# Eight PSUM banks shared out anew between score products, turns and layer 3 in a four-layer cross-attention kernel

## What is computed

```python
x = L0(x, ctx)      # inorm, 1x1 convs, softmax(Mn^T Mm) over 256 channels, Ml A, conv Wo, + x
x = L1(x, ctx)      # 32 query heads, 8 key heads of 8; softmax; out @ Wo + x; layernorm
x = L2(ctx, x)      # latents = x; 16 heads of 16 over [ctx, x]; out proj + x; rmsnorm;
                    # gelu(out @ w1 + b1) @ w2 + b2 + x
x = L3(x, ctx)      # RWKV block: token shift, mixes, r k v g w, a scan over 64 tokens
                    # for 8 x 8 states, group norm, output proj; then a channel-mix ffn
```

## Time and profile before

| | us |
|---|---|
| median of 3 runs | 1959.85 (1957.9 to 1962.85) |
| profiled execution, its span from first to last instruction | 1957.6 |
| PE busy / DVE / ACT / POOL | 1663.1 / 1235.2 / 939.7 / 812.5 |
| mean granted clock of TensorE | 0.931 of full speed |

### The profile page before, as it was taken

How to read it: one execution, slowest core, us unless ns; L and a number is a source line. 1 busy time by engine, 2 the same in 40 slices (tenths; PEclk the granted TensorE clock), 3 DMA queues, 4 the chain that set the end, 5 groups by cost and what they waited for, 6 DMA issues and landing times.

```text
span 1957.6 us, 36688 instructions
## 1 busy us (share of the span) xinstructions
PE 1663.1 (85%) x13615; PEld 1032.1 (53%) x13615; DVE 1235.2 (63%) x2121; ACT 939.7 (48%) x1855; POOL 812.5 (42%) x903
## 2 busy tenths in 40 slices
PE   5888898889997898898987989978998889888735
PEld 3565555565563655555554645646455465556203
DVE  3743478645786468844786457854688546973483
ACT  4454554545554445545544455544555544453202
POOL 4531248404573147702485034830467113760070
PEclk8998999998999899998998989989999989999857
DMA  6001014200331005100141102310052000410070
GB/s 179 2 2 35 1 20 53 45 18 1 44 41 33 18 1 67 24 27 18 18 55 34 29 1 36 49 34 18 1 61 30 27 18 9 59 24 13 1 87 11
DMA packets 73583, 60.92 MB, mean 31 GB/s; under 512 B 38960, under 2 KB 56512, under 8 KB 73408
## 3 DMA queue, kind: packets, MB, share of 16 engines
q1 hardware_dynamic: 55648, 47.99, 17.2%
q10 hardware_dynamic: 17216, 10.55, 1.9%
q0 software_dynamic: 544, 0.03, 0.0%
HBM read 20.28 MB, written 4.19 MB: 13 GB/s over the span
## 4 chain that ended last, share of the span: by engine, by line
PE 54%; DVE 18%; ACT 10%; issue 9%; POOL 6%; DMA 1%; DVEq 0%; ACTq 0%; POOLq 0%; SPq 0%
PE bank L627 21%; PE bank L766 7%; PE bank L1008 6%; PE bank L643 4%; PE bank L899 3%; PE bank L946 2%; DVE seg_max L1472 2%; POOL soft_ring L1684 2%; ACT soft_ring L1145 2%; PE bank L971 2%; PE bank L886 2%; DVE late L1322 1%; DVE late L1310 1%; PE bank L706 1%; PE bank L781 1%
## 5 line engine op out<-in xcount | busy, mean ns | idle before, releaser
L1684 POOL TENSOR_TENSOR soft_ring<-soft_ring,seg_max 128x512 f32<-128x512 f32 x256 | 286.8, 1135 | 308.5 <-DVE seg_max L1472 307.8
L1164 ACT ACTIVATE soft_ring<-soft_ring 128x512 f32<-128x512 f32 x256 | 160.5, 627 | 195.0 <-POOL soft_ring L1684 180.9
L1310 DVE TENSOR_TENSOR_SCAN late<-late 128x520 f32<-128x520 f32 x128 | 222.4, 1738 | 35.2 <-POOL late L1640 16.5
L1638 POOL TENSOR_TENSOR late<-late 128x520 f32<-128x520 f32 x128 | 192.3, 1502 | 90.5 <-DMA late<-late 58.3
L766 PE MATMUL bank<-early 32*128 32x128 f32 (+2 forms) x1024 | 155.2, 422 | 50.7 <-ACTq L1148 46.4
L946 PE MATMUL bank<-ident,soft_ring 128*128 128x128 f32 x1024 | 164.4, 290 | 17.5 <-ACT soft_ring L1164 13.0
L1472 DVE TENSOR_REDUCE seg_max<-soft_ring 128x8 f32<-128x512 f32 (+1 forms) x256 | 167.0, 676 | 6.8 <-DVE early L1522 2.1
L946 PEld LDWEIGHTS bank<-ident,soft_ring 128*128 128x128 f32 x1024 | 116.0, 145 | 93.7 <-issue 57.4
L1692 POOL TENSOR_SCALAR soft_ring<-soft_ring,rden 128x256 f32<-128x256 f32 x64 | 61.8, 966 | 239.4 <-DVE rden L1430 239.4
L1036 ACT ACTIVATE late<-bank 128x512 f32<-128x512 f32 (+2 forms) x104 | 62.0, 596 | 166.2 <-PE bank L627 162.9
L627 PE MATMUL bank<-early,w 128*128 128x512 f32 x256 | 119.8, 619 | 18.4 <-ACT early L1226 18.4
(11 more groups left out here) (255 smaller groups left out, 3348.5 us busy)
## 6 DMA issues: line engine op xcount, KB each, us to landing
late<-late SPq DMA_DIRECT2D x128, 260.0 KB, 4.4
c<-in_ctx ACTq DMA_DIRECT2D x8, 512.0 KB, 4.0
x<-in_x ACTq DMA_DIRECT2D x8, 512.0 KB, 4.9
out_x<-late SPq DMA_DIRECT2D x8, 512.0 KB, 2.9
mask<-in_mask_Bx1xSxS_ff ACTq DMA_DIRECT2D x16, 128.0 KB, 3.9
mask<-in_mask_BxS_ik SPq DMA_DIRECT2D x8, 256.0 KB, 3.2
w<-in_L_xattn_mlp_w SPq DMA_DIRECT2D x2, 1024.0 KB, 9.8
wkv<-in_L_xattn_kv_w SPq DMA_DIRECT2D x1, 512.0 KB, 3.8
```

The costliest lines, as they stand in the source:

```text
L1164: af(soft[:, u % SOFT, :], soft[:, u % SOFT, :], ACT.Exp).then_inc(sig("exp"), 1)
L1310: nc.vector.tensor_tensor_scan(sj[:, n % 2, :], wP[:, k, :, :].rearrange("p b t -> p (b t)"), aj[:, n % 2, :], 0.0, ALU.mult, ALU.add).the ...
L1638: tt(aj[:, n % 2, :], kP[:, k, :, :].rearrange("p b t -> p (b t)"), vj[:, n % 3, :], ALU.mult).then_inc(sig("kv_done"), 1)
L1684: tt(s, s, seg_max[:, u % SOFT, 0:segs].unsqueeze(2).broadcast_to([128, segs, 512 // segs]), ALU.subtract).then_inc(sig("sub"), 1)
```

## The change

The ring for scores gets four banks (0 to 3) and the ring "turn" two (4 and 5); layer 3 keeps 6 and 7. The products "mm", "mn", "ml", "k1", "v1", "q1", "q2", "k2", "v2" and "u" move from the ring "turn" to the ring "score". The turned tiles (cT, t0, x1T, t, lT, xnT), the attended values (o0, attended) and the outputs (x1, out, y2) stay in "turn". Of 102 fills of "turn" in a group 28 move, so that 74 share two banks where 102 shared four, and 68 share four where 40 shared two. No instruction is added or removed but waits on other semaphores.

```diff
-        RINGS = {"score": [0, 1], "turn": [2, 3, 4, 5], "late": [6, 7]}
+        RINGS = {"score": [0, 1, 2, 3], "turn": [4, 5], "late": [6, 7]}
...
-                    product(("mm", q), 512, [(conv["Wm"][:, :], ch[:, 2 * q:2 * q + 2, :])])
+                    product(("mm", q), 512, [(conv["Wm"][:, :], ch[:, 2 * q:2 * q + 2, :])], "score")
...
-                    t, full = fill(pe, "turn", ("ml", q))
+                    t, full = fill(pe, "score", ("ml", q))
...
-                    t, full = fill(pe, "turn", "k1")
+                    t, full = fill(pe, "score", "k1")
...
-                    t, full = fill(pe, "turn", ("q2", q))
+                    t, full = fill(pe, "score", ("q2", q))
...
-                        t, full = fill(pe, "turn", ("v2", p))
+                        t, full = fill(pe, "score", ("v2", p))
...
-                    product(("u", n), 512, [(w1[:, k, 128 * n:128 * n + 128], xnT[:, :, k, :]) for k in range(KT)])
+                    product(("u", n), 512, [(w1[:, k, 128 * n:128 * n + 128], xnT[:, :, k, :]) for k in range(KT)], "score")
```

More of the change, by code:

```diff
@@ L741, in tensor_program @@
                 for q in range(2):
-                    product(("mm", q), 512, [(conv["Wm"][:, :], ch[:, 2 * q:2 * q + 2, :])])
+                    product(("mm", q), 512, [(conv["Wm"][:, :], ch[:, 2 * q:2 * q + 2, :])], "score")
                 for q in range(2):
-                    product(("mn", q), 512, [(conv["Wn"][:, :], xh0[:, 2 * q:2 * q + 2, :])])
+                    product(("mn", q), 512, [(conv["Wn"][:, :], xh0[:, 2 * q:2 * q + 2, :])], "score")
                 step()
                 for q in range(2):
-                    t, full = fill(pe, "turn", ("ml", q))
+                    t, full = fill(pe, "score", ("ml", q))
                     for p in range(2):
@@ L861, in values1 @@
                 def values1():
-                    t, full = fill(pe, "turn", "v1")
+                    t, full = fill(pe, "score", "v1")
                     for b in range(NB):
@@ L870, in queries1 @@
                     pe.wait_ge(sig("x1T_ready"), past("x1T_ready") + h + 1)
-                    t, full = fill(pe, "turn", ("q1", h))
+                    t, full = fill(pe, "score", ("q1", h))
                     for g in range(GQ):
@@ L891, in keys2 @@
                     for h in range(KT):
-                        product(("k2", h, q), 512, [(kv[:, 0, k, 128 * h:128 * h + 128], hT[:, k, 4 * q:4 * q + 4, :, :]) for k in range(KT)])
+                        product(("k2", h, q), 512, [(kv[:, 0, k, 128 * h:128 * h + 128], hT[:, k, 4 * q:4 * q + 4, :, :]) for k in range(KT)], "score")
                 def values2(q):
                     for p in (2 * q, 2 * q + 1):
-                        t, full = fill(pe, "turn", ("v2", p))
+                        t, full = fill(pe, "score", ("v2", p))
                         for b in range(2):
```

## The result

The changed kernel takes 2021.1 us (median of 4 runs, 2019.7 to 2022.8) against 1961.1 us of the kernel before beside it (4 runs, 1957.9 to 1962.9): ratio 1.031, 95% interval 1.0296 to 1.0325. It is 60 us slower. The profiled execution's span is 2018.7 us, 61.1 us over the 1957.6 us of before.

The account below looks back on a forecast made before the run. PE was taken as the bound, busy 1663.1 of 1957.6 us. Terms 2.4 + 2.1 + 1.3 - 0.4 - 0.6 = 4.8 us lost a group, 38 over eight, gave 1996, plus 2.2 for the median: 1998 us, range 1966 to 2040.

Parts of the forecast that it names:

- The sign: Whole kernel: the change makes it slower, by 1.9%; chance of slower 0.79, same 0.07, faster 0.14.
- the mechanism: Layers 0 to 2: turn fills on two banks wait for drains queued behind other engine work; 5.8 us a group lost.
- The two late tiles of layer 0: Layer 0: sixth turned tile and x1T wait for DVE to drain attended tiles, 2.0 and 2.4 us late.
- The move of the products: Products sharing four banks with scores: costed at nothing, since the fill four back is long drained; otherwise about 0.6 us a drain.
- Forecast 2.4 us lost a group: Layer 0, net of score gain and turn loss: 2.4 us lost a group, bounds 5.1 gained and 4.4 lost.
- 4.4 lost less 2.4 gained: Layer 0: late turned tile and x1T lose 2.0 + 2.4 us; earlier results on ACT gain 2.4 us.
- the 5.1 us of bank waits: Layer 0 scores, group 4: waits of 3.31 and 1.81 us go; 2.4 us gained, 2.7 us become data waits.
- 2.4 + 2.1 + 1.3 - 0.6 a group: Losses a group in layer 0, end of layer 1, end of layer 2, less waits saved at later scores and v2.
- -3.2 us for the clock: End of layer 1: shorter waits might leave the clock up for the query products; 0.4 us a group taken back.
- the two waits that I put at 5.5 and 3.1 us: End of layer 2: a turn 5.5 us late for ACT's drain, xnT 3.1 us late for DVE's; 1.3 us lost net.
- the 0.6 a group that I took back for the waits at v2 and the later scores: Later scores and v2: bank waits of 1.2 us a group go, half lying before data waits; 0.6 us gained.
- The 0.1 us for a semaphore: End of layer 1: DVE's add after the second output product comes 2.0 us late, 2.1 with the semaphore.

Follow-up runs that it names:

- Experiments 1 and 2: Kernel before, turned tiles, attended values, outputs, lT, xnT of layers 1 and 2 on two banks: 2051.2 us; instead layer 0's turned, attended, x1, x1T: 2001.7 us.
- 12: Changed kernel with turned tiles (t0, t) and turned halves (x1T, lT, xnT) moved to the ring of four: 1956.7 us, ratio 0.997.
- experiments 9 and 10: Kernel before with four score banks and two turn banks, no product moved: 2121.3 us; changed kernel with the rings of before, products moved: 2070.4 us.
- The ring of six: Kernel before with scores, products, turned tiles, attended values and outputs all on one ring of six banks, layer 3 keeping two: 1943.2 us, ratio 0.991.
- six_layer0: Kernel before with only layer 0's tiles and k1 on one ring of six banks; layers 1 and 2 keep two and four: 1946.1 us, ratio 0.992.
- narrow_layer0: Kernel before with only layer 0's turned tiles, attended values, x1 and x1T on two banks, scores keeping two: 2001.7 us, ratio 1.021.
- three_three: Changed kernel with three banks in each ring, score and turn, instead of four and two: 1993.0 us, ratio 1.016 to the kernel before.
- rings_only: Kernel before with four banks for scores and two for turns, the products staying in the turn ring: 2121.3 us, ratio 1.081.

## Why the prediction was right, and what in it was not

The sign, the range and the mechanism held. The size was off: 38 us forecast, 60 measured.

**Right.** Each wait named for the changed profile is there: L946 for ACTq L1176 51.1 us, L812 for DVEq L1482 18.3, L812 and L781 for DVEq L1435 14.9 and 14.5; that of L766 for ACTq L1148 is gone; busy times are within 0.5% but for POOL's (1.3% less). The two late tiles of layer 0 were forecast 2.0 and 2.4 us late and waited 1.76 and 2.07. "x1T" came 34.3 us after the first scores of group 4 instead of 32.2. Experiments 1 and 2 show each loss without the other part of the change, and 12 shows that nothing else was lost: with turned tiles and halves off the two banks, the kernel takes no longer than before.

The move of the products cost nothing, as costed; experiments 9 and 10 show what lies uncovered, far more than the 0.6 us a fill that I named.

**Right in the sum, not in its parts: layer 0.** Forecast 2.4 us lost a group, measured 2.1 in group 4 (43.4 us instead of 41.3) and 16.0 in groups 1 to 7, 2.3 a group. The first group, which I counted like the others, got 2.9 us shorter. But the parts are +3.75 us of idle time (9.23 instead of 5.48) and -1.65 us of busy time, the granted clock being 0.96 instead of 0.88. I had 4.4 lost less 2.4 gained because the results come earlier; that is 2.0, and I wrote 2.4, so 3 us of the 38 are a slip. And of the 5.1 us of bank waits I expected 2.7 back as waits for data; 3.08 + 1.40 = 4.5 came. The ring of six, which has the gain without the losses, shows the same: its layer 0 is 2.4 us shorter in group 4, exactly my number, but of that 2.2 is busy time (33.64 instead of 35.82) and only 0.2 idle. So the 5.1 us of bank waits came back as waits for data nearly whole, and whether it was ACT's earlier results or PE's higher clock that made layer 0 shorter, these runs don't settle.

**Mis-sized terms.** Over eight groups my terms were 41.6 us of idle time (2.4 + 2.1 + 1.3 - 0.6 a group) and -3.2 us for the clock; the measured are 54.2 and +7.1. Of the idle time, layer 0 had 23.8 instead of 19.2, layer 1 20.0 instead of 16.8, layer 2 10.4 as forecast (with some luck: the two waits that I put at 5.5 and 3.1 us were 3.50 and 1.27 in group 4), and of the 0.6 a group that I took back for the waits at v2 and the later scores nothing is seen, though those waits are gone: 4.6 + 3.2 + 0 + 4.8 is the 12.6 us that idle time was short. What made layer 0's and layer 1's terms larger, the runs don't settle. The 0.1 us for a semaphore stood in no row; in the changed kernel PE went on 0.2 us after DVE's drain had ended (947.43 to 947.63). End of layer 1 and layer 2 lost 4.9 us a group (18.4 + 20.4 over eight), 6.0 with the stretch between them, at the edge of the 6 that I had named as wrong in size. A group took 238 us, not 234.

**The step that failed is the clock's.** I credited 0.4 us a group at the end of layer 1 and looked no further. There the clock did rise to 1.00, and the eight query products took 1.99 us; over layer 1 it gave 1.6 us of the 3.2. But layer 2 then ran slower, and that term, 19.4 us of busy time in its two stretches, stood at 0 in my sum; with layer 0's -10.7 and layer 1's -1.6 it makes the +7.1. Group 4 shows where, in stretches of about 5 us of the changed kernel (columns as in the earlier trace rows):

```profile
1035.50:1040.00 4.50, 3.74 (x34) 2.14 (x32) 4.26 (x9) 0.35 (x1) 4.36 (x7) 1.00 0.69 84
1040.00:1044.50 4.50, 1.76 (x10) 1.44 (x12) 3.47 (x9) 2.05 (x5) 4.42 (x6) 0.71 0.32 39
1044.50:1049.70 5.20, 5.20 (x31) 3.35 (x28) 4.79 (x7) 2.90 (x6) 2.36 (x2) 0.59 0.00 0
```

PE ran at full clock until it waited 3.03 us for an exponential before 1042.74, and then at 0.71 and 0.59; sixteen score matmuls took 2.08 us instead of 1.16. In the kernel before the low clock came behind the 3.02 us wait for "lT", and the same place of layer 2 had two waits of 1.39 and 1.77 us and no fall. In six_layer0 the 3.03 us wait for "lT" (before 973.40) and its low clock are there as before:

```profile
967.00:972.00 5.00, 3.04 (x72) 2.39 (x71) 4.58 (x10) 3.45 (x9) 4.41 (x5) 1.00 0.32 37
972.00:977.00 5.00, 3.34 (x11) 2.74 (x12) 4.65 (x6) 2.35 (x5) 3.03 (x4) 0.62 0.91 100
977.00:982.00 5.00, 5.00 (x12) 3.00 (x11) 4.79 (x5) 2.40 (x5) 4.63 (x4) 0.70 0.69 80
```

and a second fall came behind a wait of 2.33 us at 1001.04. This second fall goes with the +9.7 us of six_layer0 and the +9.2 of narrow_layer0: behind a wait of 1.70 to 2.47 us in the first half of layer 2 the clock over the next 5 us was 0.58 to 0.71 in each of groups 1 to 7 of both kernels, and behind 1.37 to 1.78 us in the same stretch it was 1.00 in each of them in the kernel before. How long the wait is doesn't decide it. The same four transposes, group 4 of the kernel before and then group 6 of six_layer0:

```profile
1012.99 0.66 PE L812 MATMUL bank<-ident,c 128*128 128x128 f32 x4 [1.77 <-DVE c L1498]
```

```profile
1465.14 1.11 PE L812 MATMUL bank<-ident,c 128*128 128x128 f32 x4 [1.70 <-DVE c L1498]
```

The first ran at 1.00 behind 1.77 us, the second at half of it behind 1.70. Elsewhere too: 2.40 us before the mlp's first product (385.36 in the kernel before) left the clock at 1.00, 2.42 us before the same product at 1072.23 was followed by 0.66 over 5 us. What sets a fall off, and why the waits of layer 2 fuse in the changed kernel, stays open.

The Trainium skill ("Perfetto Trace Analysis", section "Optimization Strategy") says that a gap that repeats on the engine to be saturated can mean too few buffers for the next tile. The scores' waits agreed with it as a diagnosis: with more banks all 46.4 us went. The section names no price, and the one that I read into it, all 46.4 us back, did not hold: in the ring of six, layer 0's idle time, where these gaps were, fell by 6.8 us.

## What to carry to other kernels

A ring of banks must be as deep as the drains are late, and a drain is late by whatever its in-order engine has queued ahead of it. Count the fills on a ring, and whose drains they wait for: in layer 1 six fills a round on two banks, with drains by two engines, cost 20 us; the four that ACT drains, or the two others, cost 4 us alone. One common ring of six banks did better than any split by kind that was tried (0.991; the best split 0.997), and made in layer 0 alone it was worth as much (0.992). Taking a bank wait away gives back only what the data behind it allows.

A forecast for PE needs its busy time at the clock it will run at, stretch by stretch: nearly half of the error here (10.3 of 22.9 us) is busy time, which moved with the low clock.

## What the runs showed of the hardware

The low clock moved from one stage to another without any instruction of PE changed: in the first half of layer 2, 8.5 to 18.8 us more busy time in ten of the twelve experiments and 8.4 in the changed kernel, while its idle time changed by -7.6 to +4.9. Busy time made up half of what three_three lost by its span, 36.5 us (busy +18.4 over the four stretches, idle +16.9). Layer 0's busy time fell by 3 to 17 us in all kernels but narrow_layer0 and rings_only. Waits of nearly the same length (1.77 and 1.70 us) before the same instructions were followed by a granted clock of 1.00 in one kernel and of 0.70 over 5 us in the other. A bank came back as late as its draining engine's queue made it: PE waited 1.76 and 2.07 us for drains of 0.47 and 0.48 us by DVE.
